# Four graph layers on one core: GpSimd's waits for landed transfers dropped, and the last layer's exponentials and shares kept in PSUM

## The reference

```python
# layer 0: graph convolution, a weighted segment sum
msg = h[src] * coef[:, None];  agg = segment_sum(msg, dst)
# layer 1: two edge convolutions (1a, 1b), a segment maximum each
msg = x[src] @ W_msg + edge_attr @ W_edge
agg = segment_max(msg, dst);   c = leaky_relu(agg + x @ W_root + b)
# layer 2: softmax aggregation
m = relu(feat[src]) + EPS;     a = exp(m - seg_max[dst]) / denom[dst]
out = (feat + segment_sum(a * m, dst)) @ W + b
# layer 3: attention with a loop at every node
e = leaky_relu(a_src[src] + a_dst[dst], 0.2)
alpha = exp(e - m[dst]) / (denom[dst] + 1e-16)
out = tanh(segment_sum(h[src] * alpha[:, None], dst) + bias)
```

## Time and profile before

| | |
|---|---|
| median of the runs | 3968.76 us |
| the profiled execution | 3985.76 us, its span 3983.8 us |
| GpSimd (POOL) | busy 2730.4 us, 69% of the span, 2760 instructions |
| VectorE (DVE) | busy 2817.0 us, 71% |
| TensorE (PE), ScalarE (ACT) | busy 1869.8 us and 1854.5 us, 47% each |
| `entry` with the placing | from 155.7 to 640.1 us |
| layer 0 | from 640.1 to about 1157 us |
| layer 1a, layer 1b | from 1157 and 1715 us |
| layer 2 | from 2309 to 2921 us |
| layer 3 | from 2921 us to the end |

### The profile page before, as it was taken

How to read it: one execution, slowest core, us unless ns; L and a number is a source line. 1 busy time by engine, 2 the same in 40 slices (tenths; PEclk the granted TensorE clock), 3 DMA queues, 4 the chain that set the end, 5 groups by cost and what they waited for, 6 DMA issues and landing times. The chain is left out here.

```text
span 3983.8 us, 39751 instructions
## 1 busy us (share of the span) xinstructions
PE 1869.8 (47%) x8382; PEld 1372.5 (34%) x8382; DVE 2817.0 (71%) x10490; ACT 1854.5 (47%) x3815; POOL 2730.4 (69%) x2760
## 2 busy tenths in 40 slices
PE   5478663878766666644434438887720000000000
PEld 2244213777755555522212237777720000000000
DVE  8899984888856666658887868888755555555555
ACT  8699402776642222224444436666643333333333
POOL 7366666777746777656666556676557777777776
PEclk9899755888867777766666656666755555555555
DMA  1111594665546666545665535555422222222221
GB/s 51 52 37 37 139 288 123 164 172 158 155 126 194 190 187 207 185 130 185 183 188 181 166 125 176 165 178 172 151 76 78 78 71 78 78 70 78 78 70 52
DMA packets 380539, 524.64 MB, mean 132 GB/s; under 512 B 221914, under 2 KB 255983, under 8 KB 380042
## 3 DMA queue, kind: packets, MB, share of 16 engines
q1 hardware_dynamic: 286154, 366.89, 27.9%
q0 software_dynamic: 94144, 155.21, 16.4%
HBM read 230.36 MB, written 291.54 MB: 131 GB/s over the span
## 5 line engine op out<-in xcount | busy, mean ns | idle before, releaser
L1630 POOL DMA_INDIRECT l_G<-t,src x391 | 389.6, 996 | 200.8 <-issue 108.8
L1930 POOL DMA_INDIRECT l_G<-t,src x391 | 408.3, 1044 | 168.1 <-issue 104.9
L1309 POOL DMA_INDIRECT l1b_G<-t,src x391 | 378.9, 969 | 203.1 <-issue 111.0
L1309 POOL DMA_INDIRECT l1a_G<-t,src x391 | 377.8, 966 | 191.7 <-issue 113.1
L2163 PE MATMUL l_psR<-l_diag,l_ones 128*128 128x128 f32 x2 | 0.8, 502 | 1039.7 <-DVE l_diag L2027 1039.7
L1945 POOL DMA_INDIRECT out<-O,nidx x392 | 397.8, 1015 | 128.3 <-issue 118.6
L642 POOL DMA_INDIRECT O<-x_pad,nidx x344 | 326.4, 949 | 149.8 <-issue 98.3
L973 POOL DMA_INDIRECT l_G<-xs,src x327 | 312.5, 956 | 99.7 <-issue 97.2
L2163 PEld LDWEIGHTS l_psR<-l_diag,l_ones 128*128 128x128 f32 x2 | 0.5, 311 | 1039.8 <-DVE l_diag L2027 1039.8
L207 ACT ACTIVATE O<-O,l_shift,l_rstd 128x96 f32<-128x96 f32 x784 | 291.2, 453 | 27.2 <-DVE l_shift L201 27.2
L1482 PE MATMUL l1b_psE<-l1b_G,ident 128*128 128x384 f32 (+1 forms) x198 | 144.6, 832 | 318.9 <-DMA l1b_G<-t,src 318.9
(11 more groups left out here) (350 smaller groups left out, 6511.6 us busy)
## 6 DMA issues: line engine op xcount, KB each, us to landing
h<-l_G SPq DMA_DIRECT2D x96, 392.0 KB, 2.4
t<-l1b_t_out SPq DMA_DIRECT2D x48, 768.0 KB
h<-l_G SPq DMA_DIRECT2D x48, 768.0 KB, 3.6
xs<-en_y SPq DMA_DIRECT2D x48, 392.0 KB, 3.6
t<-l_t_out SPq DMA_DIRECT2D x48, 392.0 KB, 4.0
l_H<-t SPq DMA_DIRECT2D x48, 392.0 KB, 3.2
en_y<-x_pad SPq DMA_DIRECT2D x48, 384.0 KB, 5.0
t<-l_tr_out SPq DMA_DIRECT2D x48, 384.0 KB
```

The lines of the kernel that those rows point to most:

```text
L1309: pool.indirect_dma_start(tile(c)[:, q, :], None, table, bass.IndirectOffsetOnAxis(k.src[:, at:at + 1], 0))\
L1630: pool.indirect_dma_start(tile(c)[:, q, :], None, table, bass.IndirectOffsetOnAxis(k.src[:, at:at + 1], 0))\
L1930: pool.indirect_dma_start(tile(c)[:, q, :], None, t4, bass.IndirectOffsetOnAxis(k.src[:, at:at + 1], 0))\
```

## The change

Three waits on GpSimd go: `entry`'s wait before every second block becomes a wait for the block eight before (same semaphore of the ring), and the waits for `gathered` in `layer1` and `layer2` are deleted. In `layer3`, `ex` and `share` become parts of a new PSUM tile `psK`; since the chain needs its factor as a per-partition scalar, that one of the four exponentials is copied to a small SBUF tile `fade` first, one more VectorE instruction in a step.

```diff
             for c in range(LATE):
-                if c >= 2 and c % 2 == 0:
-                    pool.wait_ge(placed[(c - 1) % RING], 128 * ((c - 1) // RING + 1))
+                if c >= RING:
+                    pool.wait_ge(placed[c % RING], 128 * (c // RING))
                 if c == HELD_BACK:
...
             for c in range(NL):
                 s = c % SLOTS
-                if c and c < NCH and c % (4 if first else 2) == 0:
-                    pool.wait_ge(gathered.of(c - 1), gathered.by(c - 1))
                 if SLOTS <= c < NCH:
...
             for c in range(NL):
                 s = c % SLOTS
-                if 1 <= c < NCH and c % 2 == 0:
-                    pool.wait_ge(gathered.of(c - 1), gathered.by(c - 1))
                 if SLOTS <= c < NCH:
...
-        ex = sb("ex", [128, 2, 4, Q])
+        fade = sb("fade", [128, 2, Q])
         mx = sb("mx", [128, 2, Q])
-        share = sb("share", [128, 2, 2, Q])
...
-        psR, psX, psF = ps("psR"), ps("psX"), ps("psF")
+        psR, psX, psF, psK = ps("psR"), ps("psX"), ps("psF"), ps("psK")
+        ex = psK[:, 0:2 * 4 * Q].rearrange("p (u i q) -> p u i q", u=2, i=4)
+        share = psK[:, 2 * 4 * Q:2 * 6 * Q].rearrange("p (u i q) -> p u i q", u=2, i=2)
...
                 dve.wait_ge(exped, c + 1)
+                dve.tensor_copy(fade[:, u, 0:n], ex[:, u, 0, 0:n])
                 dve.tensor_tensor(S[:, :, 0:W3], S[:, :, 0:W3],
                                   ex[:, u, 1, 0:n].unsqueeze(2).to_broadcast([128, n, W3]), ALU.mult)
...
-                        done = dve.scalar_tensor_tensor(S[:, q, 0:W3], before, ex[:, u, 0, q:q + 1], S[:, q, 0:W3],
+                        done = dve.scalar_tensor_tensor(S[:, q, 0:W3], before, fade[:, u, q:q + 1], S[:, q, 0:W3],
                                                         ALU.mult, ALU.add)
```

## The result

The changed kernel took **3789.70 us** in the median of four runs (3788.51 to 3792.93), the kernel before beside it 3969.27: a ratio of **0.9545**, 95% interval 0.9529 to 0.9562. The forecast was 3780, with 3738 to 3830 as the range. In the later sessions with the experiments, on two chips, the kernel before took 3976 to 3978 us; the changed kernel, run again on one of them, 3789.32, which is 188.7 us less.

What follows compares the result with a forecast made beforehand. The prediction took GpSimd, issuing indirect DMAs, to set the pace. Its terms, 32 + 36 + 57 + 17 + 47 = 189 us, taken off the median of the runs gave 3780 us, with a range of 3738 to 3830.

Steps and rivals of the forecast that it cites:

- The placing: In `entry`: GpSimd gains 45 us, but SyncE's last stores end the stage at about 608, leaving 32 us.
- Layers 1a and 1b: GpSimd's removed landing waits shrink to ordinary gaps: 36 us in 1a, 57 in 1b, where VectorE is close behind.
- Layer 2: GpSimd would save 52 us by its waits, but only 17 us was expected to show.
- the ring: Layer 2: TensorE and ScalarE's cycle of mixing, output matmuls, transposes and copy, 11.64 us, said to set the pace at 1.2 GHz.
- My weighing by the share of the two clock levels: Layer 2: about a quarter of the time at the upper clock, where waits are bare; a quarter of 52 is 13 us.
- 4 us added for the first steps: Layer 2: waits of the first steps, where TensorE has nothing to do yet, add some 4 us.
- The rival that layer 2 is freed altogether: TensorE gets the upper clock for most of layer 2: 35 us more gain, 3745 us; chance 0.15.
- Layer 3: VectorE instructions with two SBUF inputs stall GpSimd's indirect DMAs; a PSUM operand ends that: 47 us.
- the split: Layer 3's gain divided: 34 us from the gathers' stalls, 13 us from the scatters' stalls at the scaling.
- What it adds: Layer 3: 51 copies into `fade`, 9 us, hidden in the 7.4 us that VectorE waits in each step.
- later landings: Transfers queue behind SyncE's stores and half of the four stages' 142 us is lost: 3851 us; chance 0.08.
- dearer issue: Without waits GpSimd's indirect DMAs take longer, up to 0.344 us apiece: 4302 us; chance 0.05, of which 0.01 about no change.

Runs made afterwards that it cites:

- the one with the three copies: The changed kernel with three small copies of the row totals in front of the share: 3798.69 us.
- the first four experiments: The kernel before with one part of the change each: placing 3945.67 us, landing waits of 1a and 1b 3888.73, of layer 2 3961.71, PSUM 3930.87.
- e5_share_only: The changed kernel with the exponentials back in SBUF and no copy into `fade`, the shares still in PSUM: 3810.41 us.
- e6_ex_only: The changed kernel with the shares back in SBUF, the exponentials still in PSUM: 3804.44 us.
- e10_share_late: The changed kernel with the shares back in SBUF and three small copies of the row totals in front of the share: 3818.82 us.
- the late kernels: The changed kernel with three small copies in front of the share, with shares in SBUF (3818.82 us) or in PSUM (3798.69 us).

## Why the prediction was right

**The placing** (32 us; 31.7 alone, 33.0 in the profiles). The step that mattered was not what GpSimd saves (45 us) but what is late next. The stage, forecast to end at 608 behind SyncE's last stores, ends at 608.1.

**Layers 1a and 1b** (93 us; 88.7 alone, 92.2 in the profiles). The rule "a wait that goes leaves the gap of 0.3 us" gave the size. In 1b the gathers run from 1641.0 to 2138.3, 10.17 us for each of 48.9 steps, inside the 10.1 to 10.4 that I named.

**Layer 2** (17 us; 15.7 alone). The size was right and one step behind it was not: "At 1.2 GHz, then, this ring already sets the pace, and GpSimd's waits are hidden in it". If that had been so, a shorter ring would have made the kernel before faster, and it changed nothing (1.0003). A few us could hide in that, since the ring's 11.64 us and GpSimd's step lie close together; but the rows on record speak against the step too. GpSimd's waits for a slot in layer 2 were ordinary gaps of 0.3 us, so the ring never held it, and the round before the one that I read, with the mixing at 2.02 us, took 11.62 us as well. What the runs show is that GpSimd with its waits set the pace, at 11.47 us a step in the mean (11.02 after), and that the ring stood some 16 us a layer behind it. My weighing by the share of the two clock levels, with 4 us added for the first steps, came out at nearly the same number by luck: no run shows either term. The rival that layer 2 is freed altogether falls: its clock after the change is 0.63, as before.

**Layer 3** (47 us; 46.5 alone, 48.7 in the profiles). The mechanism and the sum were right. What failed is the split that I built on it, 34 us for `share` and 13 for `ex`: the second held (14 us), the first came out at 10 in one kernel and 20 in another. The term of the earlier trace rows is what the stalls cost in that one alignment of the two engines; taken part by part it isn't a constant. With both operands in PSUM the gathers took 955 ns at either alignment (the changed kernel, and the one with the three copies).

**What it adds.** The 51 copies into `fade` cost nothing that can be seen: layer 3 gained all that its stalls had cost. Three more copies in each step were covered too: VectorE's wait for gathers shrank by 41.7 us (from 307.4 in the changed kernel to 265.7 with the copies), and of the 5 us that layer 3 grew, 3.9 lie at its end, behind the last gather, where nothing covers them.

**The sum** (189 us; 179.6 in the first comparison, 3978.05 - 3789.32 = 188.7 in the last). The 10 us by which the forecast missed are as much as the kernel before varies from session to session, 3969 to 3978, and I had taken the gain off its low end; the changed kernel took 3789.70 and 3789.32. The rivals of later landings and of dearer issue fall together. No group that lost its waits got longer than a microsecond in the mean, and the waits for landed gathers shrank in each layer that lost them: VectorE's from 174.5 to 139.8 us in 1a and from 39.8 to 13.5 in layer 2, TensorE's from 318.9 to 260.3 in 1b, where VectorE waits for TensorE and not for the gathers.

**Layer 0** was not touched, and in the profiles it is 8.6 us shorter. 7.6 of these lie at its end, between the last gather and the first one of 1a, 37.0 us before and 29.4 after. That gap was 33.0, 30.4, 36.9 and 30.4 us in the first four experiments, none of which touches it; it varies from one execution to the next and is no part of the gain. Why it does stays open.

## What to carry to other kernels

When a wait is removed, first ask for each stage by itself who is late next: here three stages gave the whole wait or were stopped by a store at a time that could be read off the trace, and one was stopped by a ring that stood 16 us behind. A row of waits says who sets a stage's pace more safely than one round of a ring does: an engine that never waits for a slot isn't held by the ring. Where a long `tensor_tensor` of VectorE works beside indirect DMAs of GpSimd and these are on the path, try one of its two operands in PSUM if there is room; a small tile of weights was enough here. And don't price one half of such a stall by itself from the trace of the whole: a shift of a tenth of a microsecond moves it.

## What the hardware showed that I had not expected

How long an indirect DMA is held depends on what VectorE is doing at the moment when the DMA starts. Four cases with a `tensor_tensor` of two operands in SBUF, from the rows above and the earlier trace rows (the end of VectorE's instruction is its start plus its duration):

| DMA, start | VectorE's instruction that runs | its end | DMA ends | after it |
|---|---|---|---|---|
| scatter, 3113.90 (before) | scaling, since 3113.49 | 3114.45 | 3115.29 | 0.84 us |
| gather, 3119.44 (before) | own product, since 3119.35 | 3120.30 | 3121.12 | 0.82 us |
| gather, 3112.16 (shares late) | own product, since 3111.82 | 3112.77 | 3113.60 | 0.83 us |
| gather, 3115.88 (shares in SBUF) | neighbours' product, since 3115.08 | 3116.05 | 3116.86 | 0.81 us |

The DMA ends 0.81 to 0.84 us after the instruction that ran at its start, and so is hardly held when little of that is left. The four stand for many: of all DMAs of layer 3 in the kernels with exponentials or shares in SBUF (the one before, `e5_share_only`, `e6_ex_only`, `e10_share_late`), 213 began with more than 0.2 us of such an instruction left, and every one ended 0.81 to 0.87 us after it. An instruction that begins after the DMA does not hold it, even when it begins only 0.04 us later (3110.95 against 3110.91: 0.94 us); in those kernels no DMA that began up to 0.5 us ahead of such an instruction, with none running, took more than 0.98 us. So it is the DMA's start that counts, and not its writes, as I had put it before the late kernels ran. That an instruction can begin that soon and not matter I had not expected, and it fits that the same two instructions cost 34 us in one kernel and 10 in another.

The chain's short instructions (0.34 us) also read two tensors from SBUF and did not do this: in the same four kernels the 110 DMAs that began with more than 0.2 us of one left took 0.99 us in the median. Why they differ stays open.
